# Cross-attention's head on two engines and two row halves, with a reordered last unit and a reordered norm, in a two-layer transformer kernel

## The reference

```
# layer 0, cross-attention: 8 heads of 64
q = (x @ Wq).reshape(b, n, 8, 64)
k = (context @ Wk).reshape(b, m, 8, 64)
v = (context @ Wv).reshape(b, m, 8, 64)
attn = softmax(einsum('bihd,bjhd->bhij', q, k) * 64 ** -0.5)
out = einsum('bhij,bjhd->bihd', attn, v).reshape(b, n, 512) @ Wout + bout
# layer 1, after the state-space filter y:
xt = x_text + y
h = layernorm(xt, g_ffn, b_ffn)
h = gelu(h @ W1 + b1) @ W2 + b2
```

## Time and profile before

| | |
|---|---|
| runs | 1778.01, 1781.74, 1788.07 us; median 1781.74 |
| profiled execution | 1779.03 us, of it 1777.2 us from the first to the last instruction |
| PE busy | 1661.3 us, 93% |
| DVE busy | 993.9 us, 56% |
| ACT busy | 594.0 us, 33% |
| POOL busy | 359.4 us, 20% |
| DMA | 251.46 MB, mean 141 GB/s |

### The profile page before, as it was taken

One profiled execution on the slowest core, in us unless ns is written; L12 is line 12 of the kernel. 1 busy time (PEld: TensorE's weight loads), 2 busy tenths in 40 slices (PEclk: granted clock), 3 DMA queues, 4 the chain that ended last, 5 costly groups with the idle time before them and its releaser, 6 DMA issues. The chain is left out here.

```text
span 1777.2 us, 23431 instructions
## 1 busy us (share of the span) xinstructions
PE 1661.3 (93%) x8900; PEld 1291.1 (73%) x8900; DVE 993.9 (56%) x1526; ACT 594.0 (33%) x1084; POOL 359.4 (20%) x326
## 2 busy tenths in 40 slices
PE   7799999999998989997999998989899899999996
PEld 4799999999995767864565556758686665666672
DVE  1669678677683644455999997663526520000014
ACT  4353454444531311102543433154347421111110
POOL 0521331333030020011454543300200010000010
PEclk9899999999999989998998988989999899999998
DMA  4322131223113568547263552130101297685860
GB/s 134 111 84 85 56 111 56 87 81 112 56 43 126 195 239 284 185 152 276 84 217 130 176 215 96 59 149 1 51 4 45 62 349 255 222 321 193 316 213 30
DMA packets 113045, 251.46 MB, mean 141 GB/s; under 512 B 14726, under 2 KB 44439, under 8 KB 108183
## 3 DMA queue, kind: packets, MB, share of 16 engines
q1 hardware_dynamic: 104352, 230.72, 37.3%
q10 hardware_dynamic: 6006, 10.62, 1.7%
q0 software_dynamic: 2560, 8.39, 1.4%
HBM read 230.95 MB, written 18.75 MB: 141 GB/s over the span
## 5 line engine op out<-in xcount | busy, mean ns | idle before, releaser
L415 PE MATMUL x_s_ps<-x_cxt,x_qs 128*128 128x400 f32 (+1 forms) x1152 | 244.3, 357 | 9.5 <-POOL x_qs L388 5.5
L1204 PEld LDWEIGHTS e_ps<-e_xg,e_w 128*128 128x128 f32 x1792 | 206.6, 192 | 34.0 <-issue 33.7
L441 PE MATMUL x_o_ps<-x_cx,x_pt 128*128 128x386 f32 (+1 forms) x1248 | 230.3, 343 | 0.0
L441 PEld LDWEIGHTS x_o_ps<-x_cx,x_pt 128*128 128x128 f32 (+1 forms) x1248 | 220.6, 190 | 1.4
L1204 PE MATMUL e_ps<-e_xg,e_w 128*128 128x128 f32 x1792 | 209.8, 276 | 7.3 <-issue 6.6
L415 PEld LDWEIGHTS x_s_ps<-x_cxt,x_qs 128*128 128x128 f32 x1152 | 205.4, 191 | 10.8 <-issue 10.6
L1196 PE MATMUL e_ps<-e_w,xt 128*128 128x512 f32 x352 | 160.6, 598 | 0.1
L2398 PE MATMUL x_s_ps<-x_cxt,x_qs 128*128 128x512 f32 (+1 forms) x384 | 140.7, 523 | 3.0 <-ACT x_sc L2519 1.7
L1443 DVE TENSOR_TENSOR e_y<-e_ps,e_b 128x512 f32<-128x512 f32 x20 | 13.7, 687 | 203.8 <-PE e_ps L1196 203.8
L491 DVE TENSOR_TENSOR x_pt<-x_t_ps,x_pt 128x512 fp32r<-128x512 f32 (+1 forms) x128 | 74.7, 587 | 91.4 <-ACT x_pt L581 91.1
L2398 PEld LDWEIGHTS x_s_ps<-x_cxt,x_qs 128*128 128x128 f32 x384 | 67.7, 193 | 79.0 <-issue 77.1
(11 more groups left out here) (437 smaller groups left out, 2722.2 us busy)
## 6 DMA issues: line engine op xcount, KB each, us to landing
e_w<-in_L_ffn_W SPq DMA_DIRECT2D x16, 4096.0 KB, 14.4
x_cxt<-in_ctxT SPq DMA_DIRECT2D x8, 2401.5 KB, 8.6
x_cx<-in_ctx SPq DMA_DIRECT2D x8, 2304.0 KB
e_w<-in_L_ffn_gate_up_proj SPq DMA_DIRECT2D x8, 2048.0 KB, 8.0
x_stage<-in_ctxT SPq DMA_DIRECT2D x16, 768.0 KB, 4.4
x_stage<-in_ctx SPq DMA_DIRECT2D x16, 768.0 KB, 6.3
e_w<-in_L_ffn_down_proj SPq DMA_DIRECT2D x8, 1024.0 KB, 8.9
x<-in_ctxT SPq DMA_DIRECT2D x8, 768.0 KB, 4.3
```

Source lines behind the costliest of these rows:

```text
L415: last = nc.tensor.matmul(s_ps[:, n, 0:b - a], qs[:, u % 2, p, c, :], cxt[:, q, c, a:b], start=(m + c == 0), stop=(m + c == len(PARTS) + C ...
L441: last = nc.tensor.matmul(o_ps[:, 0:WIDE], pt[0:rows, p, t, :], cx[0:rows, q, t, :], start=(t + m == 0), stop=(t + m == KT - 1 + len(PARTS ...
L1204: last = nc.tensor.matmul(u_ps[:, g % 2, a * PER + n, :], w1[:, e % PAIR, m, a * hidden + c * P:a * hidden + (c + 1) * P], xg[:, m, :], st ...
```

## The change

Six edits, in three places.

1. Head, PE: the 24 query products go pair by pair of heads and chunk by chunk, with the even head (rows 0 to 63) and the odd head (rows 64 to 127) in turn. Each half has two banks and semaphores of its own.
2. Head, copies: ACT copies the even heads' results, DVE the odd ones'.
3. Head, context: `cxt` and `qs` are allocated ahead of both blocks, and a part of the split moves into the head: ACT makes the high parts of pieces 0 and 1 between its scalings, DVE their low parts ahead of its copies, POOL the padding of `cxt`, the high parts of pieces 2 and 3 and unit 0's queries, and SP loads the first two value pieces. The low parts of pieces 2 and 3, three padding strips and unit 1's queries stay in the second block.
4. Last unit: the 13 transposes of unit 31 go into the four free score banks, with no wait for one another, ahead of the last group of `weigh(30)`. DVE makes the low parts of its first two groups before it scales unit 30, and the two filter products of that unit behind the low parts. ACT stores unit 29's result one unit later.
5. Layer 1's norm: by_act is 2, so tile 2 is made by DVE as well as tile 3; the two rows are made ahead of the first weights' low parts. Statistics lie in `junk`.
6. The 14 transposes of the identity move from the feed-forward to the end of `mixing`'s PE stream, into a bank that is free by then.

```diff
+        def low_key(dve, b, n):
+
+            slot, high, low = piece(n)
+            dve.wait_ge(high_ready, b * PIECES + n + 1)
+            nc.vector.tensor_tensor(low, slot, high.bitcast(F32), ALU.subtract).then_inc(lowt_ready, 1)
...
@@ head, sync @@
+                    for n in range(2):
+                        sp.wait_ge(lowt_ready, n + 1)
+                        load(sp, 0, GR + n)
@@ head, tensor @@
                     for n in range(H * CC):
-                        h, c = n // CC, n % CC
-                        lo = (h % 2) * DH
-                        pe.wait_ge(qt_ready, h // 2 + 1)
+                        pair, c, half = n // 2 // CC, n // 2 % CC, n % 2
+                        lo = half * DH
+                        pe.wait_ge(qt_ready, pair + 1)
                         if n >= 4:
-                            pe.wait_ge(qp_used, n - 3)
...
+                            pe.wait_ge((even_used, odd_used)[half], n // 2 - 1)
+                        nc.tensor.matmul(ps[:, 4 + n % 4, :], wkt[lo:lo + DH, pair, c * P:(c + 1) * P],
+                                         qt[lo:lo + DH, pair, :], start=True, stop=True
+                                         ).then_inc((even_ready, odd_ready)[half], 1)
@@ head, scalar @@
+                        if m in (1, 2):
+                            high_part(act, 0, m - 1)
+                    for n in range(H * CC // 2):
+                        act.wait_ge(even_ready, n + 1)
+                        nc.scalar.copy(qp[:, n % CC, n // CC * 2, :], ps[:, 4 + n % 2 * 2, :]).then_inc(even_used, 1)
+                @block.vector
+                def _(dve):
+                    low_key(dve, 0, 0)
+                    low_key(dve, 0, 1)
+                    for n in range(H * CC // 2):
+                        dve.wait_ge(odd_ready, n + 1)
+                        nc.vector.tensor_copy(qp[:, n % CC, n // CC * 2 + 1, :], ps[:, 5 + n % 2 * 2, :]).then_inc(odd_used, 1)
+                @block.gpsimd
+                def _(pool):
...
+                    pool.wait_ge(lowt_ready, 2)
+                    for n in range(2, GR):
+                        slot, high, _ = piece(n)
+                        pool.wait_ge(piece_in[n], 16)
+                        nc.gpsimd.tensor_copy(high, slot).then_inc(high_ready, 1)
+                    pool.wait_ge(even_used, CC)
+                    pool.wait_ge(odd_used, CC)
+                    queries(pool, 0)
@@ units, tensor @@
+                            if u == N_UNITS - 2 and g == GR - 1:
+                                for n in range(GR):
+                                    turn(u + 1, n)
@@ units, vector @@
+                        final = u == N_UNITS - 1
...
+                        if final:
+                            filters.product(dve, 3, 0)
+                            filters.product(dve, 3, 1)
                         if slot == 7:
                             filters.total(dve, i, 3)
+                        if u == N_UNITS - 2:
+                            low_weights(u + 1, 0)
+                            low_weights(u + 1, 1)
                         dve.wait_ge(o_ready, (u + 1) * GR)
@@ layer 1 @@
-            norm = Centred(core, aside, "n5", y, xn, TT - 1)
+            norm = Centred(core, aside, "n5", y, xn, 2)
@@ mixing, tensor @@
+                for n in range(IDLE):
+                    nc.tensor.transpose(ps[:, 0, (n % KC) * P:(n % KC + 1) * P], core.ident[:, :], core.ident[:, :])
@@ feed_forward @@
-                norm.pool_minus(pool, TT - 2)
...
-                    if t == TT - 1:
-                        for n in range(IDLE):
-                            nc.tensor.transpose(tps[:, t, n % KC, :], ident[:, :], ident[:, :])
...
-                norm.act_total(act, TT - 2)
...
-                norm.act_squares(act, TT - 2)
...
-                norm.act_rows(act, TT - 2)
...
-                norm.last_statistics(dve)
+                for t in range(norm.by_act, TT):
+                    norm.statistics(dve, t)
+                for t in range(norm.by_act, TT):
+                    norm.row(dve, t)
                 dve.wait_ge(forward.w1_in, 64)
                 first_low(0)
-                norm.last_row(dve)
```

More of the change, by code:

```diff
@@ L260, in load, with turned, piece, high_part @@
                 sp.dma_start(slot, source).then_inc(piece_in[n - GR], 16)
+        both = ctx.enter_context(ExitStack())
+        EVEN = CTX + CTX % 2
+        WIDE = CD + 2
+        N_UNITS = B * H // 2
+        R = H // 2
+        PARTS = ((0, 0), (1, 0), (0, 1))
+        cxt = core.sb(both, "x0_cxt", [P, 2, CC, EVEN], F32R)
+        qs = core.sb(both, "x0_qs", [P, 2, 2, CC, P], F32R)
+        pad_ready, high_ready, lowt_ready, low_ready, qh_ready, qs_ready, s_ready, most_ready, max_ready, exp_ready, inv_ready, \
+            t_ready, pth_ready, pt_ready, o_ready, o_scaled, ot_ready, ot_stored = core.sems(
+                both, "x0", "pad_ready high_ready lowt_ready low_ready qh_ready qs_ready s_ready most_ready max_ready exp_ready "
+                "inv_ready t_ready pth_ready pt_ready o_ready o_scaled ot_ready ot_stored")
+        def turned(u, g):
+            return s_ps[:, g, :] if u == N_UNITS - 1 else t_ps[:, g % 2, :]
+        def piece(n):
+            if n < GR:
+                a, b = columns[n]
+                return staged(n), cxt[:, 0, :, a:b], cxt[:, 1, :, a:b]
+            a, b = groups[n - GR]
+            rows = P if b < KT else LAST
+            return staged(n), cx[0:rows, 0, a:b, 0:CD], cx[0:rows, 1, a:b, 0:CD]
+        def low_key(dve, b, n):
+            slot, high, low = piece(n)
+            dve.wait_ge(high_ready, b * PIECES + n + 1)
+            nc.vector.tensor_tensor(low, slot, high.bitcast(F32), ALU.subtract).then_inc(lowt_ready, 1)
+        def high_part(act, b, n):
+            slot, high, _ = piece(n)
+            act.wait_ge(piece_in[n % GR], b * 32 + (16 if n < GR else 32))
+            nc.scalar.copy(high, slot).then_inc(high_ready, 1)
+        def queries(pool, u):
+            b, r = u // R, u % R
+            if u >= 2:
+                pool.wait_ge(s_ready, (u - 1) * GR)
+            source = qp[:, :, 2 * r:2 * r + 2, b * S:(b + 1) * S]
+            high, low = (qs[:, u % 2, part, :, :].rearrange("p c (h s) -> p c h s", h=2) for part in range(2))
+            if u >= 1:
+                pool.wait_ge(qs_ready, u)
+            nc.gpsimd.tensor_copy(high, source).then_inc(qh_ready, 1)
+            pool.wait_ge(qh_ready, u + 1)
+            nc.gpsimd.tensor_tensor(low, source, high.bitcast(F32), ALU.subtract).then_inc(qs_ready, 1)
         with ExitStack() as c2:
@@ L350, in _ @@
                                 load(sp, b, n)
-                        for n in range(GR):
+                        for n in range(0 if b else 2, GR):
                             sp.wait_ge(lowt_ready, b * GR + n + 1)
@@ L459, in _ @@
                                 scores(u + 1, g)
-                            turn(u, g)
+                                turn(u, g)
                         weigh(u)
@@ L566, in store_out @@
                                        ot_ps[:, 0:CC * P].rearrange("p (c h s) -> p c h s", c=CC, h=2)).then_inc(ot_stored, 1)
-                    for n in range(GR):
-                        high_part(0, n)
                     filters.step_sizes(act)
```

134 lines of the change are left out of this document (46 added, 88 removed).

## The result

The changed kernel takes 1762.76 us (median of 16 runs, 1758.12 to 1775.25), the kernel before beside it 1778.47 us (16 runs, 1766.25 to 1798.44). The medians differ by 15.7 us. The ratio is 0.9927, with a 95% interval of 0.9904 to 0.9949: 13.0 us of 1778.5, between 9 and 17. It leaves out the two executions of the kernel before that lay over 1.5% above its fastest (1794.68 and 1798.44 us). The forecast was 1766.5 us, and the sum behind it was a gain of 13.8 us.

The account below looks back on a forecast made before the run. PE runs 93% of the span, near full clock, so time is won only where it stands still or runs slower. -3.4 - 3.5 - 2.0 - 4.9 = -13.8 us gives 1765.2 or 1767.9, taken as 1766.5 us; range 1757 to 1776.

Parts of the forecast that it names:

- Products and copies: Head: alternating halves and two copying engines bring a pair of query products to 0.95 us; -3.4 us, bounds -4.5 and 0.
- the ring: Head: two PSUM banks per half, a product starting when the one two before is copied; odd half sets 0.95 a pair.
- Start of the units: Units' block: only three paddings left before the first score, PE starts after about 1.0 us; -3.5 us.
- if POOL's paddings stretch beside DVE as its split did: Start of the units: the bound in which POOL's paddings are slowed beside DVE, gain only -2.5 us.
- The clock's part: Unit 0's scores: the shorter pause spares their half-clock stretch, worth 1.5 us, counted only in the range.
- Last unit: weigh(31) starts 1.3 us earlier, and half of 1.5 us of half clock is saved; -2.0 us, bounds -2.9 and -0.5.
- Seam: Layer 1's feed-forward start: x's first column at 1169.9 instead of 1174.98, idle transposes +0.2; -4.9 us, bounds -5.6 and -3.0.
- The products keep their pace: Rival: in the head, copies or banks still hold a product to 0.60 us; -10.4 us, 1770 us; chance 0.12.
- The lower clock moves into the head: Rival: PE's brief pauses for copies bring half clock to the head; about 1778 us, no change; chance 0.08.
- The loop pays: Rival: the lower clock falls into the units' loop; with a tenth of it, +24 - 14, 1791 us; chance 0.04.
- More pauses go: Rival: both half-clock stretches, in unit 0's scores and the last unit, vanish; 1763 us; chance 0.06.
- one of the prediction's own signs of being wrong: Any stage between 550 and 1160 us, or after 1190, that is longer than before.

Follow-up runs that it names:

- r12: Changed kernel with scores waiting for cxt's padding alone and eight banks instead of four for the query products: 1764.54 us, ratio 0.9898 to the kernel before.
- r6: Changed kernel with two copying engines and banks per half, but products in the old order, three in one half, then three in the other: 1769.75 us, one execution.
- r5: Changed kernel with products in alternation, but all 24 copies on ACT: 1764.14 us, one execution.
- r8: Changed kernel where DVE waits for POOL's paddings before it makes the third low part: 1779.31 us, one execution.
- r3: Changed kernel with edit 4 (the last unit) undone: 1767.74 us, ratio 0.9932.
- r7: Changed kernel where the scores wait for cxt's padding alone and the first weighing for the other three: 1753.53 us, one execution.
- r2: Kernel before with the head's edits alone (1 to 3): 1782.43 us, ratio 1.0.
- after: The changed kernel with all six edits, here mostly its first profiled execution: 1763.11 us; median 1762.76 us, ratio 0.9927 to the kernel before.
- r9: Kernel before with edit 5 alone (by_act is 2), the 14 idle transposes where they were: 1775.62 us, one execution.
- r10: Kernel before with edit 6 alone (idle transposes at the end of mixing), tile 2 still on ACT: 1769.78 us, one execution.
- r4: Kernel before with the seam's edits alone (5 and 6): 1771.46 us, ratio 0.9966.
- r1: The changed kernel again, unaltered: 1766.14 us, ratio 0.9932. Its landmarks late in layer 1's mixture: 1514.33 to 1619.11 in the kernel before.

## Why the prediction was right

The total came out 0.8 us from the forecast by the ratio (13.0 against 13.8) and 1.9 by the medians (15.7), but not each term, and in part by luck. One term was missed by 1.5 us, another came out 0.85 larger through a clock that rose for another reason than the one given, and the prediction let all of the head's gain stay, where 4.8 us of it went again in layer 0's mixture. In the profiled pair 5.9 us that no edit is seen to bring, late in layer 1, make up for that.

**Products and copies, -3.4: measured -3.1.** The mechanism held. The pace was 0.98 a pair, where the ring had been worked out to 0.95, and r12 shows that it is the ring: with four banks to a half it is the 0.86 of PE's own passes. What the prediction gave no split of, the runs do: going back to runs of three with split banks costs 5.5 us (r6), going back to one engine 0.4 (r5). The odd result's copy on DVE was taken to be needed; overlapping copies on ACT, visible before as five in 2.54 us, would nearly have done.

**Start of the units, -3.5: measured -2.0.** This is the step that failed. The forecast let the three paddings run at full speed, "PE starts after about 1.0", and kept "if POOL's paddings stretch beside DVE as its split did" as a mere bound, of -2.5. The first of them did stretch, and the bound was too narrow by 0.5. The row was there: POOL's split beside DVE at 1.91 instead of 0.50, with the very subtraction that now stands first in the block. The 1.1 us for the paddings came from a row in which DVE still stood idle: before, they were over by 45.98, and the subtraction began at 46.39. r8 shows that 13 elements are held as long as 384. The clock's part, 1.5 us in the range, is real where it comes (r3, r7, r12), but the prediction tied it to the shorter pause, and r3 has it with the long one.

**Last unit, -2.0: measured -2.85.** The shorter pauses gave 1.3, as worked out. The other 1.5 was the half clock of the earlier trace rows, of which half was counted because "one shorter pause remains". Right in size at its bound, wrong in cause: in r2 and r3 all pauses remain and weigh(31) still takes 7.14 and 7.12 us. What r2 has in common with after is the head's edits alone. All four executions with the old head have 8.64 to 8.67 us here, all ten with the new one 7.12 to 7.15. This isn't a saving of the whole: in r2 a stretch of half clock lies right behind weigh(31), from 542.5 to 545.9, and in all but three of the ten the longer one follows in layer 0's mixture.

**Seam, -4.9: measured -5.4, less 0.17 at the barrier.** Right, step by step: statistics 0.83 us a tile (0.9 forecast), the first column 5.29 us after the start (5.6 forecast). r9, r10 and r4 show the two edits' parts: 4.4 us from the norm alone, 3.0 from the transposes alone, 5.4 together, for they stand partly in each other's cover. The transposes at the end of `mixing` ran at full clock (1.75 us), so they cost the barrier 0.17 instead of up to 1.7.

**The rivals.** "The products keep their pace" fell with the first view of after. "The lower clock moves into the head": PEclk is 1.00 from 29 to 41 us in after, although PE waits for a bank at every second pair; the Trainium skill's report of a clock that oscillates in kernels that cycle through PSUM banks ("TensorE: Matmul & The Clock Gate", section "A second HAM failure mode: psum-queue depth-cycling") doesn't show here. "The loop pays" fell too: 454 us of it at 1.00. "More pauses go" came half true: weigh(31) is at full clock, unit 0 isn't (0.80). A thing that no rival named is that the lower clock moves to another stage: in after 17.1 us of it lie in layer 0's mixture, from 622 on, against 6.8 from 633 on before. With it one of the prediction's own signs of being wrong came true, a stage between 550 and 1160 that is longer than before (25.6 us against 20.8).

**What stays open.** Why two executions of one kernel take one or the other course in layer 1's cross-attention: that the pause of 6.7 us and the place of the half clock come with it is shown, what decides between them isn't. The long selection rounds in some executions (16.5 to 23.6 us for 15.15) were seen and not explained. The rise of the lead by 6.5 us behind the seam lies mostly in layer 1's mixture (5.9 us between the landmarks given under r1), where a stretch of lower clock of before (6.8 us at 1599) is missing in after. It goes with no edit: before, r3, r5, r6 and r9 take 103.8 to 104.8 us there, the nine others 98.0 to 98.9, r4 and r10 with the old head among them. And the totals don't show what the head is worth: none by itself (r2, at most 6.6 us), while head and seam together are worth 12 us (r3, and r1 with edit 4) and the seam alone 6 (r4) beside the same runs of the kernel before, each give or take 6. The three local gains are shown, their sum in the total is argued.

## What to carry to other kernels

In these traces two-pass float32 products of 64 rows overlap only with products in the other half of the rows: put the halves in strict turn, and give each half as many banks as cover the way from result to copy and back; a second copying engine matters far less. Ahead of a first matmul, look at what it waits for rather than at what is made: a wait for paddings that only a later step reads cost 2.5 us, and a tiny POOL instruction was as slow as the two-input DVE subtraction that it started beside. And judge small edits by the landmarks of their own place, which repeat to 0.1 us, because spans of one kernel differ by 14 us; but follow the lead into the stages behind as well, for 4.8 us won at the head were lost again in a stage that nobody had touched.

## What the runs showed of the hardware

ACT's copies of 128x512 float32 from PSUM follow each other at 0.49 us, though one alone lasts 0.59. Twelve pairs of 64-row products took 10.6 us in the two halves with eight banks, 17.3 in runs of three with four (r6). A tiny POOL instruction (13 elements a partition) took 0.22 us alone and 1.84 beside a two-input DVE subtraction. Behind a pause of PE of 6.73 us, the last products of layer 1's cross-attention ran at half clock and took 7.7 us more (18.25 us for 78 products, against 10.54); r12 had half clock on the same products after a pause of under 1 us, so the pause isn't shown to be the cause. The interval that holds them had two usual lengths, 102 and 110 us, in thirteen of fourteen executions. The shorter one came with a lower-clock stretch of PE beside work that DVE bounds. How long the same 36 products of unit 0 took after the same pause of 3.5 us differed from 6.83 to 9.60 us.
